# The drive of three of twelve scan units as a product of turned dt*u and diagonal B matrices

## The chip, the cores and the metric

The kernel runs on one core of one Trainium2 chip. The metric is the device time of one execution in microseconds (us), the median over runs. The core has five engines that run side by side, each through its own list of instructions in order: TensorE (PE in the profile, PEld for its weight loads), VectorE (DVE), ScalarE (ACT), GpSimd (POOL), and SyncE (SP), which here only issues DMAs. They meet through semaphores.

## The reference

Eight images of 64 x 64 pixels with 96 channels go through two residual blocks. The time lies in the first one, a selective scan in four directions (K), over L = 4096 positions, for 192 channels d and 16 states n:

```python
def step(h, inp):
    ul, dl, Bl, Cl = inp
    dA = jnp.exp(dl[..., None] * A)
    h = dA * h + (dl * ul)[..., None] * Bl[:, :, None, :]
    y = jnp.einsum('bkdn,bkn->bkd', h, Cl)
    return (h, y)
_, ys = lax.scan(step, h0, (u_t, d_t, B_t, C_t))
```

Here `dl` is a softplus of a projection of the input (dt), `ul` the input u, and B and C are projections too. I call exp(dl*A) the **decay** and (dl*u)*B the **drive**. A normalisation, a convolution and a projection stand ahead of it; behind it come a layer norm, a gate, a projection, and the second block (resampling and a two-layer network with a quadratic).

## The kernel before

Three phases follow one another: `pre_phase` (to about 0.6 ms), `scan_phase` (to about 10.6 ms) and `post_phase`. The change is in `scan_phase` (L309) and in constants that it reads.

**Steps and units.** A step is (image, direction, chunk of TC = 1024 positions, half of the channels): 8 x 4 x 4 x 2 = 256 steps. An even step n and the odd step n+1 are the two halves of one chunk c. A step has 12 units. A unit is 1024 positions for 128 pairs (32 channels, 4 states): channel block j = 0..2, state group g = 0..3. I write x for the unit's place in its step, 0 to 11. Before, g = x // 3 and j = x % 3.

**What one unit takes.**
- the decay, on ScalarE (`exp`, L734): exp of `dlr` (dt, broadcast over states by DMA), scaled by A. It goes to one of 3 buffers `E`.
- the drive. For g = 0..2 (9 of 12 units, x = 0..8) TensorE spreads the group's B over 128 partitions into the PSUM buffer `P[un % 2]` with two matmuls (`fill`, L588 and `spread`, L573), and VectorE multiplies it there by `dur` (dt*u, broadcast by DMA; `multiply`, L651). For g = 3 (x = 9..11, "pooled") GpSimd multiplies `dur` by a copy of B in SBUF (`brep`) into `dbu` (L796), and the decay goes to `P[un % 2]` instead.
- the scan itself, on VectorE: `H = decay*H + drive` along the 1024 positions (`scan`, L671); the last element is carried to the next chunk by ScalarE (`carry`, L740).
- the weighting with C, on GpSimd: `HC = H * crep` (`weigh`, L804), and the sum over states on TensorE (`sum_y`, L609): for each three units and each half of the positions three matmuls with 32 output partitions each, into `yps`.

**What else a step takes.** TensorE projects the chunk (`project`, L557, in even steps) and makes dt (`delta`, L567); ScalarE copies the first (L695, L696) and applies softplus to the second (L705, with a table load on either side); VectorE subtracts once a chunk (`split`, L645); GpSimd makes `dlu` = dt*u (L789); five replicas a chunk (four of C into `crep`, one of B into `brep`) are spread by TensorE (`rep`) into the PSUM area `stage` and copied by ScalarE (L714, L718). `stage` has one job at a time: the table `held` gives for each job the semaphore of the copy that freed it.

**What sets the order.** Each engine has a hand-written loop over un with the jobs placed by x. TensorE issues `fill(un + 1)` first in round un, after `scan_done` says that scan un-1 is done, since that frees `P[(un + 1) % 2]`; then `sum_y` (in two of three rounds) and the job of that x. A block of code that waits holds all behind it on its engine. `H` has 4 buffers, `HC` 7.

## Time and profile before

| | |
|---|---|
| median of 3 runs | 12532.51 us (12529.21 to 12533.41) |
| the profiled execution | 12534.78 us, its span 12533.0 us |
| VectorE busy | 11316.5 us, 90% of the span |
| GpSimd busy | 10322.3 us, 82% |
| TensorE busy | 9868.2 us, 79% |
| ScalarE busy | 6751.2 us, 54% |
| mean granted TensorE clock | 0.759 |

The span is the time from the first to the last instruction; the 1.8 us to the execution's time lie around it. A line of the profile names an engine, a line of the kernel, what it writes and reads, how often, its busy time, the mean of one in ns, and the idle time ahead of it with what ended most of that. The stretch from 2000 to 4000 us, used below, lies wholly in the scan.

### The profile page before, as it was taken

Reading aid. Unit: us, or ns where it says so; the run is one execution under the profiler, and the core shown is the slowest. Engines: PE = TensorE matmul, PEld = TensorE weight load, DVE = VectorE, ACT = ScalarE, POOL = GpSimd, SP = SyncE. Lnnn points to the kernel's source line nnn. Section 1 sums busy time; section 2 is a strip of 40 time slices with the busy share of each in tenths; the row PEclk is TensorE's granted clock in tenths of the full one; section 3 lists DMA queues with packets and bytes.
Section 4 is the critical chain, followed back from the end, with each engine's and each line's share of the span. In section 5 each row is a group of like instructions: output and inputs, shape, how many; then the busy total and the mean of one; then the engine's idle time right before and its main releaser. Section 6 shows DMA issues by size and latency. Waiting matters only on the chain. (4 is left out here: it accounts for less than half of the span.)

```text
span 12533.0 us, 125914 instructions
## 1 busy us (share of the span) xinstructions
PE 9868.2 (79%) x38648; PEld 4005.4 (32%) x38648; DVE 11316.5 (90%) x7318; ACT 6751.2 (54%) x8834; POOL 10322.3 (82%) x4494
## 2 busy tenths in 40 slices
PE   8877777777777777777777777777777776799999
PEld 5622222222222222222222222222222221578878
DVE  7789999999999999999999999999999998555554
ACT  3355555555555555555555555555555554444443
POOL 2189999999999999999999999999999998433330
PEclk9966777677767776777677767776777676799999
DMA  3333343334333333343334333433343333221220
GB/s 106 110 110 112 121 133 112 114 123 133 112 113 120 130 111 114 123 130 112 112 121 130 111 113 121 130 112 116 122 130 111 113 122 105 70 67 48 62 62 11
DMA packets 371523, 1356.57 MB, mean 108 GB/s; under 512 B 47174, under 2 KB 47750, under 8 KB 367532
## 3 DMA queue, kind: packets, MB, share of 16 engines
q1 hardware_dynamic: 370860, 1348.51, 33.5%
q8 instruction: 320, 5.24, 0.2%
q14 instruction: 343, 2.81, 0.1%
HBM read 983.43 MB, written 364.90 MB: 108 GB/s over the span
## 5 line engine op out<-in xcount | busy, mean ns | idle before, releaser
L804 POOL TENSOR_TENSOR HC<-H,crep 128x1024 f32<-128x1024 f32 x3072 | 7196.9, 2361 | 380.1 <-DVE H L671 374.3
L573 PE MATMUL psum<-sx,selb 96*128 96x512 f32 x5888 | 2902.8, 590 | 2096.8 <-DVE H L671 1447.0
L671 DVE TENSOR_TENSOR_SCAN H<-E,car,psum 128x1024 f32<-128x1024 f32 x1728 | 4055.5, 2347 | 61.7
L609 PE MATMUL psum<-HC,sely 128*32 128x512 f32 x12288 | 2957.9, 813 | 9.9 <-POOL HC L804 9.9
L573 PEld LDWEIGHTS psum<-sx,selb 96*128 96x128 f32 x5888 | 1233.2, 256 | 5190.2 <-issue 4295.4
L651 DVE TENSOR_TENSOR psum<-dur,psum 128x1024 f32<-128x1024 f32 x2304 | 2782.0, 1207 | 44.0 <-PE psum L573 43.6
L734 ACT ACTIVATE E<-dlr,am 128x1024 f32<-128x1024 f32 x2304 | 2625.7, 1146 | 322.1 <-DVE H L671 316.6
L796 POOL TENSOR_TENSOR dbu<-dur,brep 128x1024 f32<-128x1024 f32 x768 | 1818.0, 2367 | 0.0
L734 ACT ACTIVATE psum<-dlr,am 128x1024 f32<-128x1024 f32 x768 | 858.7, 1118 | 1653.3 <-DVE H L671 1645.2
L740 ACT COPY car<-H 128x1 f32<-128x1 f32 x2304 | 424.1, 184 | 1891.0 <-DVE H L671 1885.3
L671 DVE TENSOR_TENSOR_SCAN H<-E,psum 128x1024 f32<-128x1024 f32 x576 | 1317.3, 2287 | 21.4 <-ACT E L734 1.5
L671 DVE TENSOR_TENSOR_SCAN H<-psum,car,dbu 128x1024 f32<-128x1024 f32 x576 | 1309.4, 2328 | 3.1
L567 PE MATMUL psum<-dlt,dtw 6*96 6x512 f32 x1024 | 833.5, 957 | 331.2 <-DVE sx L645 330.0
L609 PEld LDWEIGHTS psum<-HC,sely 128*32 128x32 f32 x12288 | 370.6, 125 | 1450.2 <-issue 1304.1
L557 PE MATMUL psum<-u,wx 96*102 96x512 f32 x1024 | 782.9, 900 | 30.1 <-DMA u<-scr_xa 30.1
L789 POOL TENSOR_TENSOR dlu<-dlt,u 96x1024 f32<-96x1024 f32 x256 | 673.1, 2629 | 126.1 <-ACT dlt L705 126.1
L714 ACT COPY crep<-psum 128x1024 f32<-128x1024 f32 x512 | 514.8, 1005 | 164.6 <-PE psum L573 163.7
L1453 POOL TENSOR_TENSOR y<-y,tmp 96x1024 f32<-96x1024 f32 x64 | 194.8, 3089 | 459.2 <-DMA tmp<-scr_yk 459.2
L567 PEld LDWEIGHTS psum<-dlt,dtw 6*96 6x96 f32 x1024 | 210.7, 231 | 787.5 <-DVE sx L645 457.6
L1179 PEld LDWEIGHTS psum<-w2s,hs 128*100 128x100 f32 x4800 | 447.3, 168 | 15.2
L1179 PE MATMUL psum<-w2s,hs 128*100 128x96 f32 x4800 | 447.8, 252 | 0.0
L1464 POOL TENSOR_TENSOR y<-y,szt 96x512 f32<-96x512 f32 x128 | 163.4, 1296 | 323.3 <-ACT y L1342 281.6
(126 smaller groups left out, 9334.5 us busy)
## 6 DMA issues: line engine op xcount, KB each, us to landing
dur<-scr_dlu SPq DMA_DIRECT2D x768, 512.0 KB, 5.3
dlr<-scr_dl SPq DMA_DIRECT2D x768, 512.0 KB, 6.6
scr_dl<-dlt SPq DMA_DIRECT2D x256, 384.0 KB, 3.8
scr_dlu<-dlu SPq DMA_DIRECT2D x256, 384.0 KB, 3.0
scr_yk<-yt SPq DMA_DIRECT2D x256, 384.0 KB, 8.1
yp<-scr_yk SPq DMA_DIRECT2D x128, 384.0 KB, 3.6
scr_xa<-xs SPq DMA_DIRECT2D x64, 384.0 KB, 3.5
scr_sz<-xs SPq DMA_DIRECT2D x64, 384.0 KB, 3.4
```

The lines of the kernel that those rows point to most:

```text
L557: r = e.matmul(stage[0:C + NR, sub * 512:(sub + 1) * 512], wx[:, k, h, :], view(k, h, t0, 512), start=h == 0, stop=h == 1)
L567: r = e.matmul(stage[0:C, sub * 512:(sub + 1) * 512], dtw[C:C + NR, k * ND + half * C:k * ND + (half + 1) * C], dts[:, sub * 512:(sub + 1) ...
L573: r = e.matmul(o[:, sub * 512:(sub + 1) * 512], selb[:, which, :], sx[:, c % 2, sub * 512:(sub + 1) * 512], start=True, stop=True)
L609: r = e.matmul(yps[32 * j:32 * j + 32, cols], sely[:], HC[:, (3 * i + j) % NHC, cols], start=g == 0 and k == 1, stop=g == NG - 1)
L651: e.tensor_tensor(P[un % 2], dur[:, slot(m, j), :], P[un % 2], ALU.mult).then_inc(mul_done)
L671: e.tensor_tensor_scan(H[:, un % NH, ::step], decay[:, ::step], drive[:, ::step], init, ALU.mult, ALU.add).then_inc(scan_done)
L714: e.copy(crep[:, i, :], stage).then_inc(rep_out)
L734: e.activation(o, dlr[:, slot(m, j), :], ACT.Exp, scale=am[:, ae:ae + 1]).then_inc(exp_done)
L789: e.tensor_tensor(shaped(dlu[:], k), shaped(dl, k), view(k, half, t_of(k, ci), TC), ALU.mult).then_inc(dlu_made)
L796: e.tensor_tensor(dbu[:, j, :], dur[:, slot(m, j), :], brep[:], ALU.mult).then_inc(pool_mul_done)
L804: e.tensor_tensor(HC[:, un % NHC, :], H[:, un % NH, :], crep[:, g, :], ALU.mult).then_inc(hc_done)
L1179: r = e.matmul(o[0:NU, i * C:(i + 1) * C], hs[:, q % 2, j, i * NU:(i + 1) * NU], w2s[:, j, :], start=j == 0, stop=j == 2)
```

## The change

Of twelve units of a step, seven now take the drive as before (`DIRECT`), two are `POOLED` (in group g = 1), and three (group g = 3) are `DIAGONAL`: TensorE forms the whole drive. For that
- dt*u of the step (`dlu`, 96 channels x 1024 positions) is turned on TensorE, 128 positions at a time, into `stage` (`turn_dlu`, eight matmuls), and copied by ScalarE into `dluT` (128 x 768);
- the four B rows of group 3 are turned once a chunk (`turn_b`, eight matmuls, a copy of 128 x 32 into `blt`), and ScalarE writes 32 matrices of 128 x 128 a chunk, the identity with its rows scaled by B (`diagonal`);
- `fill` of a diagonal unit is 32 matmuls (8 blocks of 128 positions x 4 states), each with `dluT` (128 x 32) as the weights and a diagonal matrix (128 x 128) as the moving side, writing 32 partitions x 128 of `P`. VectorE's `scan` reads `P` as it is.

To have a state's 32 channels side by side, partitions are now ordered (state, channel) and no longer (channel, state), in the DMAs' broadcast, `selb`, `sely` and `alog`. `ORDER` places the groups so that units without a VectorE multiply alternate with direct ones; of even steps x = 3, 5 are pooled and 7, 9, 11 diagonal, of odd steps 1, 3, 5 are diagonal and 9, 11 pooled. `dbu` has two buffers instead of three. Jobs of `stage` and GpSimd's `delta` have other places, and `dynamic_dma_scratch_size=1024` is given.

```diff
+    NBLK = TC // 128
+    GPOOL, GDIAG = 1, 3
+    DIRECT, POOLED, DIAGONAL = 0, 1, 2
+    ORDER = ((0, 0, 0, 1, 1, 1, 2, 3, 2, 3, 2, 3), (0, 3, 0, 3, 0, 3, 2, 2, 2, 1, 1, 1))
+    KIND = tuple(tuple(DIAGONAL if g == GDIAG else POOLED if g == GPOOL and x in pooled else DIRECT for x, g in enumerate(row))
+                 for row, pooled in zip(ORDER, ((3, 5), (9, 11))))
+    REPS = (0, None, 3, 1, 2)
...
     def tensor(e):
...
+        def turn_b(c):
+            e.wait_ge(*held["bt", c])
+            e.wait_ge(sx_split, c + 1)
+            for k in range(NBLK):
+                r = e.matmul(stage[:, 4 * k:4 * k + 4], sx[:, c % 2, k * 128:(k + 1) * 128], selb[:, 2 * GDIAG, 0:128:32],
+                             start=True, stop=True)
+            r.then_inc(bt_done)
+
+        def turn_dlu(m, sub):
+            if sub == 0:
+                e.wait_ge(*held["lt", m])
+                e.wait_ge(dlu_made, m + 1)
+            for k in range(NBLK // 2):
+                t0 = (sub * (NBLK // 2) + k) * 128
+                r = e.matmul(stage[:, sub * 512 + k * C:sub * 512 + (k + 1) * C], dlu[:, t0:t0 + 128], idn[0:C, 0:C],
+                             start=True, stop=True)
+            if sub:
+                r.then_inc(lt_done)
 
         def fill(un):
-            if un >= NUNIT or on_pool(un):
+            if un >= NUNIT or kind(un) == POOLED:
                 return
-            m, g = un // 12, un % 12 // 3
-            e.wait_ge(sx_split, m // 2 + 1)
+            b, k, ci, half, m, g, j = place(un)
             if un >= 2:
                 e.wait_ge(scan_done, un - 1)
-            spread(P[un % 2], m // 2, 2 * g).then_inc(fill_done)
+            if kind(un) == DIRECT:
+                e.wait_ge(sx_split, m // 2 + 1)
+                spread(P[un % 2], m // 2, 2 * g).then_inc(fill_done)
+            else:
+                e.wait_ge(lt_copied, m + 1)
+                e.wait_ge(diag_made, NBLK * 4 * (m // 2 + 1))
+                for i in range(NBLK):
+                    for q in range(4):
+                        r = e.matmul(P[un % 2][32 * q:32 * q + 32, i * 128:(i + 1) * 128],
+                                     dluT[:, m % 2, i, 32 * j:32 * j + 32], diag[:, i, q, :], start=True, stop=True)
+                r.then_inc(fill_done)
...
             if n % 2 == 0:
-                if x < 3 and n and n < NSTEP:
+                if x < 3 and n:
                     rep(c - 1, x + 2)
-                if x in (4, 7) and c < NCHUNK:
-                    project(c, x // 7)
-                if x == 10 and c < NCHUNK:
+                if x in (3, 4):
+                    turn_dlu(n + 1, x - 3)
+                if x in (5, 7) and c < NCHUNK:
+                    project(c, (x - 5) // 2)
+                if x == 9 and c < NCHUNK:
                     delta(n + 2)
-            else:
-                if x == 4 and c < NCHUNK:
+            elif c < NCHUNK:
+                if x == 1:
+                    turn_b(c)
+                if x == 3:
                     delta(n + 2)
-                if x in (8, 10) and c < NCHUNK:
+                if x in (6, 7):
+                    turn_dlu(n + 1, x - 6)
+                if x in (8, 10):
                     rep(c, (x - 8) // 2)
...
     def scalar(e):
...
+        def diagonal(c, first, n):
+            if first == 0:
+                e.wait_ge(bt_copied, c + 1)
                 if c:
-                    e.wait_ge(pool_mul_done, 3 * 2 * c)
-                e.copy(brep[:], stage).then_inc(rep_out)
+                    e.wait_ge(fill_done, fills(last_of(2 * c - 1, kinds=(DIAGONAL,))) + 1)
+            for i in range(first, first + n):
+                e.mul(diag[:, i // 4, i % 4, :], idn[:], blt[:, i:i + 1]).then_inc(diag_made)
...
-            if x == 1 and 2 <= n + 1 < NSTEP and not ends_image(n + 1):
-                delta(n + 1)
-            if x in (3, 5, 7):
-                multiply(n, (x - 3) // 2)
-            if x == 7 and n + 2 < NSTEP and ends_image(n + 2):
-                delta(n + 2)
+            if n % 2 == 0:
+                if x in (0, 2):
+                    multiply(12 * n + 3 + x)
+            else:
+                if x == 0 and n + 1 < NSTEP:
+                    delta(n + 1)
+                if x in (3, 5):
+                    multiply(12 * n + 6 + x)
+                if x == 8 and n + 2 < NSTEP:
+                    delta(n + 2)
```

TensorE's list at the middle of an even step, before. `psum<-sx,selb` is a spread, `psum<-u,wx` a half of `project`, `psum<-yp,idn` and `psum<-HC,sely` belong to `sum_y`, `psum<-dlt,dtw` is `delta`.

```order
L573 MATMUL psum<-sx,selb 128x512 x2
L557 MATMUL psum<-u,wx 102x512 x2
L573 MATMUL psum<-sx,selb 128x512 x2
L603 MATMUL psum<-yp,idn 96x512
L609 MATMUL psum<-HC,sely 32x512 x3
L573 MATMUL psum<-sx,selb 128x512 x2
L603 MATMUL psum<-yp,idn 96x512
L609 MATMUL psum<-HC,sely 32x512 x3
L573 MATMUL psum<-sx,selb 128x512 x2
L557 MATMUL psum<-u,wx 102x512 x2
L609 MATMUL psum<-HC,sely 32x512 x6
L567 MATMUL psum<-dlt,dtw 96x512 x2
```

The same place after the change, from round x = 3 of an even step on (`psum<-idn,dlu` is `turn_dlu`, `psum<-diag,dluT` the fill of a diagonal unit):

```order
L624 MATMUL psum<-idn,dlu 128x96 x8
L601 MATMUL psum<-sx,selb 128x512 x2
L659 MATMUL psum<-yp,idn 96x512
L665 MATMUL psum<-HC,sely 32x512 x3
L585 MATMUL psum<-u,wx 102x512 x2
L643 MATMUL psum<-diag,dluT 32x128 x32
L659 MATMUL psum<-yp,idn 96x512
L665 MATMUL psum<-HC,sely 32x512 x3
L601 MATMUL psum<-sx,selb 128x512 x2
L585 MATMUL psum<-u,wx 102x512 x2
L643 MATMUL psum<-diag,dluT 32x128 x32
```

The first half of `project` now stands behind the spread and the first `sum_y` of the step and directly ahead of a diagonal fill; so does the second half.

ScalarE's list in the first half of an even step, before (`E<-dlr,am` is `exp`, `car<-H` a carry, `yt<-psum` the copy of y):

```order
L718 COPY brep<-psum 128x1024
L734 ACTIVATE E<-dlr,am 128x1024
L740 COPY car<-H 128x1
L746 COPY yt<-psum 96x1024
L734 ACTIVATE E<-dlr,am 128x1024
L740 COPY car<-H 128x1
L734 ACTIVATE E<-dlr,am 128x1024
L740 COPY car<-H 128x1
```

After:

```order
L824 ACTIVATE psum<-dlr,am 128x1024
L830 COPY car<-H 128x1
L836 COPY yt<-psum 96x1024
L808 ACTIVATE diag<-idn,blt 128x128 x2
L824 ACTIVATE E<-dlr,am 128x1024
L830 COPY car<-H 128x1
L808 ACTIVATE diag<-idn,blt 128x128 x2
L799 COPY dluT<-psum 128x768
L824 ACTIVATE E<-dlr,am 128x1024
L830 COPY car<-H 128x1
L808 ACTIVATE diag<-idn,blt 128x128 x2
```

Diagonal matrices stand in each round here, and the copy of `dluT` behind them in round x = 5; the last two matrices of the chunk are in round x = 6.

## Rows read from the trace of the kernel before

**Rows 1.** The page: span, and busy time of each engine.

```profile
span 12533.0 us, 125914 instructions
PE 9868.2 (79%) x38648; PEld 4005.4 (32%) x38648; DVE 11316.5 (90%) x7318; ACT 6751.2 (54%) x8834; POOL 10322.3 (82%) x4494
```

**Rows 2.** The page: TensorE's granted clock in 40 slices of the span.

```profile
PEclk9966777677767776777677767776777676799999
```

**Rows 3.** Windows of the scan: length, busy PE PEld DVE ACT POOL, clock, DMA, GB/s.

```profile
2000.00:4000.00 2000.00, 1503.85 (x4204) 438.96 (x4202) 1977.25 (x1105) 1143.86 (x1472) 1926.28 (x823) 0.71 0.35 117
5031.50:5038.00 6.50, 6.24 (x10) 2.90 (x10) 6.43 (x5) 3.39 (x5) 6.50 (x4) 0.50 0.80 257
5038.50:5045.00 6.50, 6.41 (x28) 2.07 (x31) 6.43 (x4) 1.43 (x3) 6.50 (x4) 1.00 0.20 61
```

**Rows 4.** The page: the multiply on VectorE, over the whole span.

```profile
L651 DVE TENSOR_TENSOR psum<-dur,psum 128x1024 f32<-128x1024 f32 x2304 | 2782.0, 1207 | 44.0 <-PE psum L573 43.6
```

**Rows 5.** Groups of instructions from 2000 to 4000 us.

```profile
L804 POOL TENSOR_TENSOR HC<-H,crep 128x1024 f32<-128x1024 f32 x617 | 1445.8, 2361 | 73.7 <-DVE H L671 72.5
...
L651 DVE TENSOR_TENSOR psum<-dur,psum 128x1024 f32<-128x1024 f32 x462 | 557.8, 1207 | 3.8 <-PE psum L573 3.7
L734 ACT ACTIVATE E<-dlr,am 128x1024 f32<-128x1024 f32 x460 | 524.3, 1146 | 60.4 <-DVE H L671 59.2 <-issue 0.2
L796 POOL TENSOR_TENSOR dbu<-dur,brep 128x1024 f32<-128x1024 f32 x155 | 367.1, 2368 | 0.0
...
L789 POOL TENSOR_TENSOR dlu<-dlt,u 96x1024 f32<-96x1024 f32 x51 | 133.4, 2616 | 0.0
L714 ACT COPY crep<-psum 128x1024 f32<-128x1024 f32 x101 | 101.6, 1006 | 30.7 <-PE psum L573 30.6
L740 ACT COPY car<-H 128x1 f32<-128x1 f32 x472 | 86.9, 184 | 387.9 <-DVE H L671 386.7
```

**Rows 6.** VectorE in order of time: start, us, line, what, count.

```profile
5021.19 1.21 DVE L651 TENSOR_TENSOR psum<-dur,psum 128x1024 f32<-128x1024 f32 x1
5022.43 2.29 DVE L671 TENSOR_TENSOR_SCAN H<-E,psum 128x1024 f32<-128x1024 f32 x1
5024.64 1.21 DVE L651 TENSOR_TENSOR psum<-dur,psum 128x1024 f32<-128x1024 f32 x1
```

**Rows 7.** TensorE in order of time; in brackets the idle time ahead.

```profile
4999.65 1.93 PE L609 MATMUL psum<-HC,sely 128*32 128x512 f32 x6
...
5028.94 1.06 PE L609 MATMUL psum<-HC,sely 128*32 128x512 f32 x6
5031.76 1.19 PE L573 MATMUL psum<-sx,selb 96*128 96x512 f32 x2 [1.75 <-DVE H L671]
...
5039.42 0.74 PE L573 MATMUL psum<-sx,selb 96*128 96x512 f32 x2
5040.00 1.02 PE L603 MATMUL psum<-yp,idn 96*96 96x512 f32 x2
5040.95 1.06 PE L609 MATMUL psum<-HC,sely 128*32 128x512 f32 x6
...
5042.63 1.88 PE L557 MATMUL psum<-u,wx 96*102 96x512 f32 x4
```

**Rows 8.** Short matmuls on TensorE in the last phase, in order of time.

```profile
10978.39 0.90 PE L1137 MATMUL psum<-ut,x 64*64 64x100 f32 x16
...
11317.56 1.46 PE L1161 MATMUL psum<-ut,t 64*64 64x100 f32 x20
...
11321.09 2.81 PE L1179 MATMUL psum<-w2s,hs 128*100 128x96 f32 x30
```

**Rows 9.** Groups on ScalarE from 10800 us on, with small operands.

```profile
L1393 ACT COPY t<-psum 128x400 f32<-128x400 f32 x42 | 20.7, 492 | 72.2 <-PE psum L1137 72.2
...
L1384 ACT ACTIVATE b1a<-b1p,co 128x1 f32<-128x1 f32 x21 | 6.6, 378 | 28.1 <-DVE b1p L1275 28.1
```

**Rows 10.** Waits from 2000 to 4000 us: total us, times, longest.

```profile
DVE psum L651 <- PE psum L573: 3.7, 10, 0.6
...
DVE sx L645 <- ACT sx L696: 0.9, 2, 0.5
```

More of the change, by code:

```diff
@@ L336, in scan_phase @@
     dlu = T("dlu", [C, TC])
+    blt = T("blt", [128, NBLK * 4])
+    diag = T("diag", [128, NBLK, 4, 128])
+    dluT = T("dluT", [128, 2, NBLK, C])
     sx = T("sx", [C, 2, TC], F32R)
@@ L393, in shaped, with kind, tally, fills @@
         return ap if k % 2 == 0 else ap.rearrange("p (w h) -> p w h", h=HW)
-    def unit_of(m, g, j):
-        return 12 * m + 3 * g + j
     def place(un):
         m, x = divmod(un, 12)
-        return steps[m] + (m, x // NJ, x % NJ)
-    def on_pool(un):
-        return un % 12 >= 3 * GB
-    def a_index(un):
-        return 9 * (un // 12) + un % 12
-    def a_unit(a):
-        return 12 * (a // 9) + a % 9
+        return steps[m] + (m, ORDER[m % 2][x], x % NJ)
+    def kind(un):
+        return KIND[un // 12 % 2][un % 12]
+    def tally(un, *kinds):
+        c, r = divmod(un, 24)
+        return c * sum(KIND[p][x] in kinds for p in range(2) for x in range(12)) + sum(kind(i) in kinds for i in range(r))
+    def fills(un):
+        return tally(un, DIRECT, DIAGONAL)
+    def muls(un):
+        return tally(un, DIRECT)
+    def pooled(un):
+        return tally(un, POOLED)
+    def last_of(m, **want):
+        return max(un for un in range(12 * m, 12 * m + 12)
+                   if want.get("g", place(un)[5]) == place(un)[5] and want.get("j", un % 3) == un % 3
+                   and kind(un) in want.get("kinds", (DIRECT, POOLED, DIAGONAL)))
+    filled = [un for un in range(NUNIT) if kind(un) != POOLED]
+    pooled_units = [un for un in range(NUNIT) if kind(un) == POOLED]
     def slot(m, j):
@@ L602, in sum_y @@
                 e.wait_ge(yp_in, 16 * (seconds(m) + 1))
-                r = e.matmul(yps[0:C, cols], idn[:], yp[:, cols], start=True, stop=False)
+                r = e.matmul(yps[0:C, cols], idn[0:C, 0:C], yp[:, cols], start=True, stop=False)
                 if sub:
@@ L618, in tensor @@
         delta(0)
+        turn_b(0)
+        turn_dlu(0, 0)
+        turn_dlu(0, 1)
         delta(1)
@@ L683, in vector @@
             c = n // 2 + 1
-            if not on_pool(un):
+            if kind(un) == DIRECT:
                 multiply(un)
@@ L755, in scalar @@
         delta(0)
+        turn_b(0)
+        turn_dlu(0)
         delta(1)
@@ L760, in scalar @@
         exp(0)
+        diagonal(0, 0, 18)
         for un in range(NUNIT + 12):
@@ L766, in scalar @@
                 carry(un - 1)
+            if x == 4 and n:
+                copy_y(n - 1)
+            if n == NSTEP:
+                continue
             if n % 2 == 0:
-                if 1 <= x <= 3 and n and n < NSTEP:
+                if 1 <= x <= 3 and n:
                     rep(c - 1, x + 1)
+                if x < 7:
+                    diagonal(c - 1, 18 + 2 * x, 2)
+                if x == 5:
+                    turn_dlu(n + 1)
                 if x == 8 and c < NCHUNK:
                     project(c)
-                if x == 11 and c < NCHUNK:
+                if x == 10 and c < NCHUNK:
                     delta(n + 2)
-            else:
-                if x == 5 and c < NCHUNK:
+            elif c < NCHUNK:
+                if x == 2:
+                    turn_b(c)
+                if x == 5:
                     delta(n + 2)
-                if x in (9, 11) and c < NCHUNK:
+                if x == 7:
+                    turn_dlu(n + 1)
+                if x in (9, 11):
                     rep(c, (x - 9) // 2)
-            if x == 4 and n:
-                copy_y(n - 1)
+                if x >= 6:
+                    diagonal(c, 3 * (x - 6), 3)
     def pool(e):
```

113 lines of the change are left out of this document (70 added, 43 removed).

## The prediction, made before the changed kernel ran

> **What bounds the kernel now.** I read the page's totals first, then the windows of the scan, then the groups, then the order of time. VectorE is the busiest engine over the span [rows 1], but that is a mean over phases; from 2000 to 4000 us it is busy 1977.25 of 2000 us, GpSimd 1926.28, TensorE 1503.85, ScalarE 1143.86 [rows 3]. VectorE waits there for TensorE's fill only 3.7 us in ten places [rows 10]. So the scan phase is VectorE's own work end to end. The multiplies count the steps: 462 in 2000 us, nine a step, give 51.3 steps of 38.97 us, of which VectorE idles 0.44 us. 256 steps are 9976 us.
>
> GpSimd is close behind: twelve weightings of 2.361, three multiplies of 2.368 and one dlu of 2.616 [rows 5] are 38.1 us a step by durations. The change must take from both, and it does.
>
> TensorE is the engine to watch. Its clock stands at 0.71 in the scan [rows 3] and near 1.0 in the first and last phase [rows 2], so it runs part of the scan at 1.2 GHz and part at 2.4 (at 0.5 and 1.0, a mean of 0.71 is 58% of the time at the lower). One sum of three matmuls takes 1.93 us at the one and 1.06 at the other [rows 7].
>
> **What is taken away.** VectorE loses two of nine multiplies a step: 512 in all, by 1.207 us [rows 4], is 618 us. (By starts the multiply costs 1.24, 5021.19 to 5022.43 [rows 6]; I keep the duration.) The scans stay, and a diagonal unit reads its drive from PSUM as a direct one does. GpSimd loses one of three multiplies: 12 x 2.361 + 2 x 2.368 + 2.616 = 35.7 us a step. VectorE's new step is 38.97 - 2.41 = 36.56 us, so GpSimd stays below. Its places matter too: an odd step now has two dlu (38.3 us of work), an even one none (33.1). Followed unit by unit with starts at each scan's end, GpSimd is some 6 us behind at the end of the odd step and catches up in the even one. `H` lets it be about three units (9 us) behind, and `sum_y` two to three; I cost this at nothing, covered by the even step's slack of 3.5 us.
>
> **The diagonal fill.** 32 matmuls, fp32, so 64 instructions by the trace's habit of two records each. The nearest row is `sum_y`: six instructions of 512 columns on three sets of 32 output partitions take 1.06 us [rows 7], where four of 512 columns on one set take 1.88, or 0.43 each: the three sets work side by side, in two turns of 0.43 plus 0.2 for the way out. With four sets and 128 columns, the fill is 16 turns of 0.107 plus 0.2: 1.9 us at 2.4 GHz; at 1.2 GHz 16 x 0.213 + 0.2 = 3.6. A short-matmul row supports it: sixteen of 100 columns, two sets, 0.90 us [rows 8], (0.90 - 0.2)/8 = 0.09 a turn. I take 2.1 with its issue. The bounds: 1.8 below, and above, if the four sets go one after another, 64 x 0.107 = 6.8, near the 0.09 of L1179's instructions on one set (thirty in 2.81 [rows 8]).
>
> May it be late? The fill may start when scan un-2 ends; ahead of the scan that needs it VectorE has the direct neighbour's multiply and scan, 3.45 us by starts [rows 6]. That is what alternating the kinds does. At 2.4 GHz 2.1 fits, with 1.3 us left for whatever TensorE still has; at 1.2 GHz 3.6 does not quite.
>
> **TensorE's sum** for a step at 2.4 GHz, by spacing of starts: seven spreads of 0.6 are 4.2; three diagonal fills 6.3; eight sums of 0.95 (5040.00 to 5040.95 and the like) 7.6; skip or earlier y, two of 0.95 in three of four steps, 1.4; half a project and a delta, four instructions of 0.43 each, 3.4; two and a half replicas 1.5; `turn_dlu`, 16 instructions of 0.094, 1.5; `turn_b` 0.4. Together 26.3 of 36.6 us. At 1.2 GHz it would be about 52: more than a step. So TensorE cannot stay at the low clock; its clock in the scan must rise, to some 0.85 or 0.9 by my estimate, since the full rows after 5038.5 [rows 3] follow a dense stretch at half clock and the change makes stretches dense.
>
> **Where VectorE will wait.** Set t = 0 at the end of scan 4 in an even step. Scan 7 is due at 2.27 + 3.45 = 5.7. TensorE meets: the spread 0.65, earlier y 0.95, the sum 0.95, half of project 1.7 (it also waits for the copy of `dluT`: on ScalarE a carry 0.2, two diagonals 0.6, the copy 0.8, so 1.6 to 2.1, earlier than TensorE gets there); the diagonal fill starts at 4.3 and ends at 6.4. Wait 0.7. The next one (x = 9) has sum, spread and the other half of project ahead, 0.3 to 0.5 late; `split` 0.1; the third, behind `delta`, is saved by the split's 1.2. In the odd step each diagonal has 0.3 to 1 us to spare. That is 1.2 us for two steps at the full clock.
>
> But between rounds 3 and 5 TensorE idles about 2.6 us. After an idle time of 1.75 us the rows from 5031.76 on run at 0.50, for 6.5 us of steady work [rows 3, 7]. If that happens here, 6.5 us yield 3.3 and the fill ends at 9.6: a wait of 3.9 instead of 0.7, 4.4 in all. I take 2.3 for two steps, between these ends, because the clock was low only 58% of the time with the old density, and the denser lists should hold it up more often. 128 x 2.3 = 294 us, bounds 154 and 563.
>
> **ScalarE.** 16 diagonals a step. A copy of one column is 0.184 and of 1024 1.006 [rows 5]; a one-column ACTIVATE with operands read from a tile 0.378, a copy of 400 columns 0.492 [rows 9]. I take 0.39, about 0.3 by spacing (bounds 0.2 and 0.5): 4.8 a step, plus 0.8 for the copy of `dluT` and little else. It was 1143.86 / 51.3 = 22.3, and becomes 28 of 37 us. Hidden, as long as no copy that TensorE waits for comes late; the last two matrices are written 0.2 + 0.6 us after scan 5, before TensorE reaches fill 7. If the diagonals cost 0.5, 3 us more a step still fit. The DMAs move the same bytes with another order of rows; none is waited for by VectorE: nothing. Eighteen diagonals ahead of the first unit cost 5 us, once.
>
> **Sum.** 12534.8 - 618 + 294 + 5 = 12216 by the profiled execution; it lies 2.3 over the median, so 12214. I say 12210.
>
> **Rivals.**
> (1) The low clock at each first diagonal fill, 4.4 to 5 us for two steps: 12534 - 618 + 563 to 640, 12480 to 12556. For it: the idle 2.6 us ahead, longer than the 1.75 of the row. Against: density. It is centred on no change.
> (2) Slower: the diagonal fill is bound by its number of instructions. Twenty short ones of L1161 take 1.46 us, 0.063 each without the 0.2 [rows 8], though two sets were at work. At that pace 64 take 4.0 + 0.1. Against the window of 3.45 each fill is 0.65 late by itself; with what stands ahead of them, x = 7 is 2.7 late, x = 9 2.5, x = 11 0.5, and the odd step's 0.65, 0.65 and, behind `delta`, 2.0: 9 us for two steps, 1152 in all: 13070. It turns to slower once a fill takes about 3.1 us at the full clock. For it: no row has 64 such instructions in a run. Against: L1137's sixteen go at 0.044. Sets that don't overlap (6.8) would give 26.3 + 14.1 = 40.4 us a step on TensorE, at least 12534 + 256 x 1.4 = 12900, and belong here.
> The Trainium skill ("TensorE: Matmul & The Clock Gate", "Wait — 56ns, not 53.3ns?") has a rule for this: with hardware decoding off, the sequencer takes about 62 ns a matmul, and that binds when the array's work is shorter. By it the fill would be 64 x 62 ns = 4.0 us, an estimate, and the time this rival's. L1137's row is faster than that, but sixteen may have been decoded beforehand, so the trace doesn't settle it.
> (3) ScalarE works in order; table loads, diagonals and copies pile up, and its exp or copy is late by 1 to 2 us a step: 12214 + 256 or 512, 12470 to 12730. For it: 28 us in pieces that wait for others. Against: it has 9 us a step to spare.
> (4) All at the full clock and all hidden: 12534 - 618 + 0 to 154, 11916 to 12070.
>
> **How the numbers follow.** Forecast 0.50 (12100 to 12330), rival 4 0.10, rival 1 0.15 (a third each way), rival 3 0.09, rival 2 0.16. Faster by over 0.2% (25 us, about what a measurement can tell): 0.50 + 0.10 + 0.06 + 0.05 = 0.71; same 0.06; slower 0.23. The range holds the forecast, most of rival 4, rival 1 and more than half of 3: 11960 to 12680.
>
> **What would show it.** In the profile after: 1792 multiplies on VectorE instead of 2304, at 1.207; the diagonal's fill near 2 us from its first to its last start at clock 1.00; waits of VectorE's scan for the diagonal fill, near 0.7 us or more, once in two steps at x = 7; the clock of the scan at 0.85 or more; ScalarE near 28 us a step. The prediction is wrong if a diagonal fill takes over 3 us at the full clock, if VectorE waits at all six diagonal units of two steps, if ScalarE or GpSimd ends its waits, or if the clock stays near 0.7.

## The result, and the profile after

| | before | after |
|---|---|---|
| time, median (us) | 12,533.0 | 13,066.3 |
| lowest to highest | 12,529.2 to 12,536.1 | 13,056.9 to 13,069.2 |
| span of the profiled execution | 12,533.0 | 13,055.0 |
| granted clock from 2000 to 4000 us | 0.71 | 0.83 |

The change makes the kernel slower: the ratio is 1.0424, 95% interval 1.0406 to 1.0442, or 533 us. The prediction was 12,210 in a range of 11,960 to 12,680; both its sign and its range were wrong. The number of its slower rival, 13,070, is close to the result, but it is not that rival's mechanism: at the full clock the fills are as short as forecast.

The page of the kernel after: span, busy time, and the groups that the prediction speaks of (columns as in [rows 1, 4, 5]).

```profile
span 13055.0 us, 236757 instructions
PE 10838.8 (83%) x91896; PEld 5733.0 (44%) x91896; DVE 10740.7 (82%) x6806; ACT 8110.9 (62%) x13314; POOL 9754.9 (75%) x4238
...
L718 DVE TENSOR_TENSOR psum<-dur,psum 128x1024 f32<-128x1024 f32 x1792 | 2169.4, 1211 | 308.6 <-DMA dur<-scr_dlu 158.0
...
L808 ACT ACTIVATE diag<-idn,blt 128x128 f32<-128x128 f32 x4096 | 1375.5, 393 | 1.5 <-issue 0.8
```

VectorE does 1792 multiplies instead of 2304, as intended, and is busy 576 us less than in [rows 1]. Its idle time grew by more. L718 is the multiply (L651 before), L740 the scan (L671 before), L601 the spread, L712 the split, L643 the fill from diagonals, L808 the writing of one diagonal on ScalarE.

Waits of the kernel after from 2000 to 4000 us, all engines (total us, times, longest). In [rows 10] VectorE's whole list for the same stretch is 4.6 us.

```profile
DVE H L740 <- PE psum L643: 95.1, 40, 5.4
DVE psum L718 <- DMA dur<-scr_dlu: 33.8, 15, 4.6
DVE psum L718 <- PE psum L601: 21.8, 33, 1.2
DVE sx L712 <- ACT sx L765: 20.3, 23, 1.9
...
ACT E L824 <- DMA dlr<-scr_dl: 140.6, 59, 6.9
...
SPq L514 <- DMA scr_dlu<-dlu: 507.3, 50, 17.6
```

Two things are new. One was foreseen, with its place: the scan waits for a fill from diagonals (95.1 us, 40 times, up to 5.4). The other was not: VectorE and ScalarE wait for the broadcasts `dur` and `dlr`, and the queue that issues them waits up to 17.6 us for a write to the scratch in DRAM. The page's DMA issues (KB each, median us from issue to landing) show how long such a write takes now:

```profile
scr_dl<-dlt SPq DMA_DIRECT2D x256, 384.0 KB, 15.2
scr_dlu<-dlu SPq DMA_DIRECT2D x256, 384.0 KB, 13.1
```

The same two writes took 3.8 and 3.0 us in the kernel before. Nothing about them was changed; what was changed is what stands around them in the queues, the broadcasts. A window of 10 us of before, then one of after (columns as in [rows 3], the DMA share is the last but one):

```profile
5070.00:5080.00 10.00, 9.61 (x19) 2.70 (x16) 9.89 (x7) 8.01 (x10) 10.00 (x5) 0.50 0.95 346
```

```profile
5050.00:5060.00 10.00, 8.84 (x153) 6.51 (x150) 9.75 (x6) 4.84 (x10) 10.00 (x5) 0.83 0.24 82
```

Before, the broadcasts came in bursts on nearly all 16 DMA engines (share 0.95, 346 GB/s). In the window of after the share is a quarter, and the rate 82 GB/s. The bytes moved over the whole execution are the same.

**The fill from diagonals** itself, in TensorE's order of time in the kernel after: the first ran with the clock changing in it (granted clock 0.61 over its row), the second at 1.00, the third mostly at 0.50 (0.53).

```profile
5031.16 3.09 PE L643 MATMUL psum<-diag,dluT 128*32 128x128 f32 x64
...
5039.12 1.96 PE L643 MATMUL psum<-diag,dluT 128*32 128x128 f32 x64
...
5050.69 3.55 PE L643 MATMUL psum<-diag,dluT 128*32 128x128 f32 x64 [0.52 <-DVE H L740]
```

### The profile page after: what moved, and what is told of

Read it like the earlier page. It is cut to its first block and busy times, and to the rows that moved or that the text cites. A ratio compares the mean times of both kernels' runs of the same rounds, so it can differ in the third digit from the quotient of the medians.

```text
span 13055.0 us, 236757 instructions
## 1 busy us (share of the span) xinstructions
PE 10838.8 (83%) x91896; PEld 5733.0 (44%) x91896; DVE 10740.7 (82%) x6806; ACT 8110.9 (62%) x13314; POOL 9754.9 (75%) x4238
## 3 DMA queue, kind: packets, MB, share of 16 engines
q14 instruction: 373, 3.05, 0.1%
## 5 line engine op out<-in xcount | busy, mean ns | idle before, releaser
L740 DVE TENSOR_TENSOR_SCAN H<-E,car,psum 128x1024 f32<-128x1024 f32 x1920 | 4473.4, 2343 | 597.1 <-PE psum L643 374.8
L601 PE MATMUL psum<-sx,selb 96*128 96x512 f32 x4864 | 2161.8, 541 | 1709.9 <-DVE H L740 1114.6
L824 ACT ACTIVATE E<-dlr,am 128x1024 f32<-128x1024 f32 x2560 | 2922.2, 1146 | 1026.2 <-DMA dlr<-scr_dl 784.2
L601 PEld LDWEIGHTS psum<-sx,selb 96*128 96x128 f32 x4864 | 940.7, 237 | 3538.7 <-DVE H L740 1961.3
L718 DVE TENSOR_TENSOR psum<-dur,psum 128x1024 f32<-128x1024 f32 x1792 | 2169.4, 1211 | 308.6 <-DMA dur<-scr_dlu 158.0
L643 PE MATMUL psum<-diag,dluT 128*32 128x128 f32 x49152 | 1724.9, 300 | 166.4 <-DVE H L740 165.6
L643 PEld LDWEIGHTS psum<-diag,dluT 128*32 128x32 f32 x49152 | 1477.4, 121 | 865.5 <-DVE H L740 529.2
L740 DVE TENSOR_TENSOR_SCAN H<-E,psum 128x1024 f32<-128x1024 f32 x640 | 1453.6, 2283 | 205.4 <-PE psum L643 151.5
L808 ACT ACTIVATE diag<-idn,blt 128x128 f32<-128x128 f32 x4096 | 1375.5, 393 | 1.5 <-issue 0.8
L904 POOL TENSOR_TENSOR dbu<-dur,brep 128x1024 f32<-128x1024 f32 x512 | 1213.6, 2370 | 2.4 <-ACT brep L781 2.4
L740 DVE TENSOR_TENSOR_SCAN H<-psum,car,dbu 128x1024 f32<-128x1024 f32 x384 | 894.2, 2329 | 10.7 <-ACT psum L824 9.5
L624 PEld LDWEIGHTS psum<-idn,dlu 96*128 96x128 f32 x4096 | 558.4, 212 | 275.8 <-issue 212.4
L624 PE MATMUL psum<-idn,dlu 96*128 96x96 f32 x4096 | 600.3, 301 | 0.6 <-POOL dlu L895 0.6
## 6 DMA issues: line engine op xcount, KB each, us to landing
scr_dl<-dlt SPq DMA_DIRECT2D x256, 384.0 KB, 15.2
```

What stands on the lines that cost most here:

```text
L601: r = e.matmul(o[:, sub * 512:(sub + 1) * 512], selb[:, which, :], sx[:, c % 2, sub * 512:(sub + 1) * 512], start=True, stop=True)
L624: r = e.matmul(stage[:, sub * 512 + k * C:sub * 512 + (k + 1) * C], dlu[:, t0:t0 + 128], idn[0:C, 0:C], start=True, stop=True)
L643: r = e.matmul(P[un % 2][32 * q:32 * q + 32, i * 128:(i + 1) * 128], dluT[:, m % 2, i, 32 * j:32 * j + 32], diag[:, i, q, :], start=True, ...
L718: e.tensor_tensor(P[un % 2], dur[:, slot(m, j), :], P[un % 2], ALU.mult).then_inc(mul_done)
L740: e.tensor_tensor_scan(H[:, un % NH, ::step], decay[:, ::step], drive[:, ::step], init, ALU.mult, ALU.add).then_inc(scan_done)
L808: e.mul(diag[:, i // 4, i % 4, :], idn[:], blt[:, i:i + 1]).then_inc(diag_made)
```

## The experiments

Two causes stood open after this profile. **D**: the new order of the replicated rows. The broadcast's destination was 32 groups of 4 partitions, and is now 4 groups of 32; by this theory a transfer whose outer dimension is 4 runs on 4 of the 16 DMA engines, where 32 runs on all. **C**: the wait for TensorE at x = 7 of the even step, made large by the low clock. Against D stood a smaller scratch area for the DMA descriptors, which the change also brings (theory S in the expectations). Theory T of the expectations is C in its first wording. Two rivals of C come with e5: theory L, that it is the amount of work ahead of the fill at whatever clock, and theory A, that ScalarE's diagonals and copies are late. All ratios are to the kernel before, measured on the same chip, with a 95% interval.

### e1: the change with the old form of the broadcast

```
-  .unsqueeze(0).to_broadcast([4, 32, TC])     (in_dur and in_dlr)
+  .unsqueeze(1).to_broadcast([32, 4, TC])
```

> The changed kernel with one thing undone: the DMAs that broadcast dl and dlu into dlr and dur read 32 rows four times each, as before ([32, 4, 1024]), and no longer 4 x 32 rows. The rows land in other partitions than the rest expects, so the output is not the reference's; bytes, instructions and waits are the same. Theory D (the broadcast with 4 as its outer dimension runs on a quarter of the 16 DMA engines, and its lateness is passed on through ScalarE to TensorE): landing of scr_dl back from 15.2 us to about 4, no wait of ScalarE's exp for dlr, time 12150 to 12400. Theory S (the small scratch for DMA descriptors slows all DMAs): the stores keep 13 to 20 us to landing, time stays near 13066. Theory T (TensorE at half clock ahead of the first diagonal fill is the cause, the DMAs are a bystander): landings recover but the time stays above 12850, with waits of about 5 us before the scan at x = 7.

The rows now land in partitions that the matrices and the decay don't expect, so this kernel computes something else with the same amount of work. Measured: 12,653.3 us, ratio 1.0096 (1.0081 to 1.0111). 413 us come back. `scr_dl` lands in 3.9 us again, `scr_dlu` in 3.2, `dur` in 5.4. The time lies between the two that D alone (up to 12,400) and T alone (over 12,850) were to give: VectorE still waits 113.2 us in 2000 for the diagonal fills, up to 6.5 at a time. Both causes are at work.

### e2: the change with four plain DMAs of 32 rows for each broadcast

The counts that are waited for go with it, 64 for each broadcast instead of 16.

```
-  e.dma_start(dur[:, slot(m, j), :], S["dlu"][m % 2, 32*j:32*j+32, :].unsqueeze(0).to_broadcast([4, 32, TC]))
+  for q in range(4):
+      e.dma_start(dur[32*q:32*q+32, slot(m, j), :], S["dlu"][m % 2, 32*j:32*j+32, :])
```

> The changed kernel with each broadcast issued as four plain DMAs of 32 rows x 4 KB (24 a step instead of 6), output as the reference. Theory D: each DMA has 32 rows as its outer dimension and uses the DMA engines as before, so the time is near that of the old broadcast, 12150 to 12450; the issue takes SyncE 24 x 0.6 = 14 us of 37 a step, which could cost some of it. Theory S and theory T: near 13066.

Measured: 12,649.9 us, ratio 1.0090 (1.0075 to 1.0105), again above the 12,450 expected at most. The same bytes go to the same partitions as in the changed kernel, and the kernel is 416 us shorter. The transfers land in 3.2 and 3.6 us; no wait for a DMA is left among VectorE's in this stretch, and what is left is the other cause:

```profile
2000.00:4000.00 2000.00, 1704.87 (x14830) 791.95 (x14831) 1838.85 (x993) 1406.97 (x2348) 1791.90 (x764) 0.83 0.45 116
```

```profile
DVE H L740 <- PE psum L643: 114.8, 46, 5.4
...
DVE sx L712 <- ACT sx L765: 20.4, 24, 1.9
...
DVE psum L718 <- PE psum L601: 5.7, 18, 0.4
```

I keep e2's form in e5 to e7 and e9 to e12: it is free of cause D.

### e3: the kernel before with the smaller scratch area for descriptors

```
-  nc = _bacc.Bacc("TRN2", target_bir_lowering=False, num_devices=1)
+  nc = _bacc.Bacc("TRN2", target_bir_lowering=False, num_devices=1, dynamic_dma_scratch_size=1024)
```

> The kernel before with only dynamic_dma_scratch_size=1024 added. Theory D and theory T: 12533, within 0.2%, landings as before (3 to 8 us). Theory S: landings of 13 to 20 us and over 12700.

Measured: 12,535.1 us, ratio 1.0002 (0.9992 to 1.0011). It costs nothing.

### e4: the kernel before with only the new order of rows

```
-  .unsqueeze(1).to_broadcast([32, 4, TC])     (in_dur and in_dlr)
+  .unsqueeze(0).to_broadcast([4, 32, TC])
-  p = (d * 4 + ni).ravel()                    (the matrices that spread and sum)
+  p = (ni * 32 + d).ravel()
-  A_logs ... .transpose(3, 5, 0, 1, 2, 4)
+  A_logs ... .transpose(5, 3, 0, 1, 2, 4)
```

> The kernel before with only the new order of partitions (DMA broadcast [4, 32, 1024], selb, sely and alog to match), output as the reference. Theory D: landings of scr_dl and scr_dlu rise to 10 us and more, DMA share about 0.25 whenever a broadcast runs; a step moves 6 x 512 KB at about 100 GB/s = 31 us of 39 in one queue, so it is slower than 12533, by my estimate 12650 to 13100. Theory S: 12533. Theory T: 12533 within 0.5%, since TensorE has slack here.

Measured: 13,100.5 us, ratio 1.0455 (1.0440 to 1.0471), at the upper end of what was expected. Without one diagonal, the order of the rows alone costs the old kernel 568 us. The old kernel's TensorE has no new work here, so D stands by itself; that it is the transfers, and not the new order in the matrices, e2 shows, which keeps that order. A window from inside a broadcast of e4, and its waits in the stretch from 2000 us on:

```profile
5005.00:5010.00 5.00, 5.00 (x11) 1.20 (x10) 4.93 (x4) 4.87 (x5) 5.00 (x4) 0.50 0.25 99
```

```profile
ACT E L734 <- DMA dlr<-scr_dl: 185.2, 61, 8.7
...
DVE psum L651 <- DMA dur<-scr_dlu: 43.0, 35, 2.1
```

A share of 0.25 of 16 engines is four engines, at 99 GB/s together, some 25 each.

### e8: the change with two broadcasts of two groups

```
+  for q in range(2):
+      e.dma_start(dur[64*q:64*q+64, ...], S["dlu"][...].unsqueeze(0).to_broadcast([2, 32, TC]))
```

> The changed kernel with each broadcast as two DMAs whose outer dimension is 2 ([2, 32, 1024]) where it has one of 4. Theory D in its strict form (the number of DMA engines that work on a transfer is its outer dimension, and the transfers of the queue follow one another): a DMA share near 2/16 = 0.13 while a broadcast runs and some 60 GB/s, so a step's 3 MB take over 50 us: 15000 us or more. If two such transfers run side by side: a share of 0.25 and about 13066. If the outer dimension has nothing to do with it: 12650.

Measured in a single execution: 20,648.7 us, span 20,646.9. It moves the same bytes as e2 and puts them in the same partitions. The windows:

```profile
5020.00:5030.00 10.00, 9.68 (x62) 4.48 (x54) 9.41 (x6) 5.24 (x13) 6.87 (x4) 1.00 0.13 52
5040.00:5050.00 10.00, 4.27 (x14) 0.70 (x8) 2.49 (x2) 0.00 (x0) 4.41 (x2) 0.52 0.13 52
```

0.13 of 16 is two engines, at 52 GB/s. The number of engines follows the outer dimension: 2 gives two, 4 gives four. The two DMAs of a broadcast don't share out over other engines either, or the share would be 0.25: SyncE issues the six for `dur` in 15.50 us and waits for nothing between them, while 1.57 MB at 52 GB/s take 30, so several are under way together. In e2 each piece has 32 rows as its outer dimension and lands fast. The Trainium skill states this rule ("DMA: Bandwidth & Descriptors", "Why a DMA increments its semaphore by 16 and not by 1"): the number of engines is the largest one up to 16 that divides the slowest dimension, other than 1, of both sides, and on a hardware queue, as SyncE's is here, they are the lowest-numbered ones. The shares of e4 and e8 agree with the first half; that e8's DMAs stay on the same two engines agrees with the second, though no view here shows which two they are.

### e5: TensorE given more to do

Replicas spread three times, and the direct fills from x = 7 of an odd step to x = 5 of an even one twice. Only work is added to e2; the last spread writes what the first did.

```
-  for sub in range(2):
+  for sub in [0, 1] * times:                   # times = 3 for replicas
...
-  spread(P[un % 2], m // 2, 2 * g).then_inc(fill_done)
+  spread(P[un % 2], m // 2, 2 * g, 2 if (un % 24) >= 19 or (un % 24) < 6 else 1).then_inc(fill_done)
```

> e2 (the changed kernel with four plain DMAs for each broadcast) with TensorE given more to do where it idles: each replica is spread three times over into the same place, and the direct fills of rounds x = 7 on of odd steps and up to x = 5 of even steps twice; same output. Theory C (VectorE waits at x = 7 because TensorE comes there at 1.2 GHz after thin rounds): the granted clock in the scan rises from 0.83 to over 0.9, waits of VectorE's scan for the diagonal fill fall from 114.8 us in 2000 to under 60, time from 12650 to 12300 to 12480, though there is more work. Theory L (it is the amount of work queued ahead of that fill, at whatever clock): no gain, 12650 to 12800. Theory A (ScalarE's diagonals and copies come late): no change, within 30 us of 12650.

Measured: 12,513.2 us, ratio 0.9982 (0.9973 to 0.9992); 137 us less than e2 by work that is only added. The granted clock of the scan rose from 0.83 to 0.92, and VectorE's wait for the diagonals fell from 114.8 to 77.7 us in 2000. The direction is C's and neither L's nor A's, but the gain is smaller than C was to give (12,480 at most, a wait under 60):

```profile
2000.00:4000.00 2000.00, 1779.31 (x15911) 921.32 (x15906) 1870.53 (x1010) 1425.46 (x2387) 1826.54 (x777) 0.92 0.46 119
```

### e6 and e7: the projection moved away from the stall

e6 takes e2 and brings the halves of `project` from x = 5 and 7 to x = 3 and 4, `turn_dlu` from 3 and 4 to 9 and 10, `delta` from 9 to 7 and the split from behind scan 8 to behind scan 5, with ScalarE's copies to match. e7 adds e5's extra work to it.

```
-  if x in (3, 4): turn_dlu(n + 1, x - 3)
-  if x in (5, 7) and c < NCHUNK: project(c, (x - 5) // 2)
-  if x == 9 and c < NCHUNK: delta(n + 2)
+  if x in (3, 4) and c < NCHUNK: project(c, x - 3)
+  if x == 7 and c < NCHUNK: delta(n + 2)
+  if x in (9, 10): turn_dlu(n + 1, x - 9)
```

> e2 with the jobs of the staging area in another order in even steps: both halves of project in rounds 3 and 4, its copies and VectorE's split at x = 5, delta in round 7 (softplus at 8), the turns of dlu in rounds 9 and 10 (copy at 11), the last diagonals by x = 4; same work, same output. Theory L: nothing stands between the first sum of the step and the fill of x = 7, none between x = 7 and 9 but delta, so VectorE's waits fall by more than half: 12300 to 12450. Theory C: the work before the fill is the same in sum and still runs at the low clock, so the wait at x = 7 stays; the 0.8 us of split's wait and x = 9's go: 12480 to 12580. Theory A: depends on when ScalarE's last diagonal is written; earlier by two rounds here, so 12450 or less with ScalarE no longer late.

> e5 and e6 together. If theories C and L each hold a part, the gains add: 12100 to 12350, below both kernels. If only C holds, as e5; if only L, as e6 or slower.

Measured: e6 12,483.8 us, ratio 0.9955 (0.9940 to 0.9970), above L's 12,450 and just inside C's 12,480 to 12,580; e7 12,504.9, ratio 0.9970 (0.9960 to 0.9980), so the gains do not add. The wait for the diagonals is nearly gone in e6, and another has come: VectorE's split waits for ScalarE's copy of the projection, which TensorE gives late, at the low clock by my reading (e12 tests it). VectorE's waits in e6, then in e7:

```profile
DVE sx L713 <- ACT sx L766: 82.2, 26, 4.5
DVE H L741 <- PE psum L644: 21.1, 35, 1.6
```

```profile
DVE sx L713 <- ACT sx L766: 71.4, 26, 5.2
DVE H L741 <- PE psum L644: 32.8, 50, 2.5
```

The extra work of e5 added in e7 raised the clock of the whole execution from 0.84 to 0.91 and gained nothing: what it took from the one wait it gave to the other. I read this as work beyond what the thin places need getting in the way itself; e12 adds less and gains, but no run shows which of e7's additions is too much.

### e9: the split moved back by two units

```
-  if x == 7 and c < NCHUNK: delta(n + 2)             (e6)
+  if x == 8 and c < NCHUNK: delta(n + 2)
-  if c < NCHUNK and n % 2 == 0 and x == 5: split(c)
+  if c < NCHUNK and n % 2 == 0 and x == 7: split(c)
```

ScalarE's copies of the projection and its softplus come one unit later as well, at x = 6 and 9.

> e6 with the copies of project on ScalarE at x = 6 (was 5), VectorE's split behind scan 7 (was 5), delta in round 8 and softplus at 9 (was 7 and 8); same work and output. In e6 the waits at x = 7 went and 3.5 us a chunk appeared at the split instead. If that was only the split's place in VectorE's list, ahead of what it needs, it goes and nothing takes its place: 12483 - 128 x 3.0 = 12100, within 12060 to 12250. If TensorE's work ahead of fill 7 at the low clock is what counts wherever the split stands, the wait is back at x = 7 to 9 and the time stays at 12400 to 12500.

Measured: 12,627.9 us, ratio 1.0072 (1.0055 to 1.0089). This missed both ranges that were expected: the split's wait is gone, but 144 us are lost against e6. TensorE now stands in the way of the fills again:

```profile
DVE H L741 <- PE psum L644: 79.3, 40, 2.7
DVE psum L719 <- PE psum L602: 58.3, 23, 3.3
```

and both halves of the projection, in one row of TensorE's order of time, take 7.12 us at the low clock (3.68 in e10's row):

```profile
5072.34 7.12 PE L586 MATMUL psum<-u,wx 96*102 96x512 f32 x8
```

### e10: e9 with each replica spread twice

```
-  spread(stage, c, 2 * GPOOL if REPS[i] is None else 2 * REPS[i] + 1).then_inc(rep_done)
+  spread(stage, c, 2 * GPOOL if REPS[i] is None else 2 * REPS[i] + 1, 2).then_inc(rep_done)
```

> e9 with each replica spread twice over (five times two more matmuls a chunk), nothing else. If the low clock still costs something in e9, the clock rises from about 0.83 towards 0.87 and the time falls by 10 to 60 us; if TensorE has slack enough in e9, it is the same as e9 within 0.2%.

Measured: 12,468.5 us, ratio 0.9950 (0.9933 to 0.9967): 159 us less than e9, where 10 to 60 were expected, with nothing changed but five instructions more a step, whose result is what stood there already (1246 of L602 in 2000 us instead of 970). The granted clock in the stretch went from 0.80 to 0.87, VectorE's wait for the diagonals from 79.3 to 72.2 us and that for the spreads from 58.3 to 36.2, and the projection's row to half:

```profile
5074.90 3.68 PE L586 MATMUL psum<-u,wx 96*102 96x512 f32 x8
```

### e11 and e12: the same addition in the order of the change, and with the projection early

The edit of e10, in e2 and in e6.

> The change with its four plain DMAs of 32 rows (12,650 us) and one thing more: each replica of a C row is spread twice by TensorE, so only work is added, about 2 x 0.48 us of it per replica and 10 replicas in two steps, in the thin rounds. Theory C (what the wait at x = 7 costs is the low clock that TensorE has when it comes to the blocks of the diagonals, and more work ahead of it keeps the clock up): the granted clock of the scan rises from 0.83 to about 0.87, and the time falls by 100 to 160 us, to 12,490 to 12,550, as between the two kernels with the later split (-160) and as when the direct fills were spread twice too (-137). Rival: the work there is what is late, whatever the clock; then the added 5 us in two steps make the wait longer, and the time rises to 12,700 to 12,900. Range 12,490 to 12,620.

> The kernel with the projection early (12,484 us, where VectorE waits 4.5 us in 26 of 50 steps for ScalarE's copy of the projection, which TensorE gives late at the low clock, and little for the diagonals), with each replica spread twice and nothing else changed. Theory C: with the clock held up ahead of the projection, that copy comes 1.5 to 2 us sooner; 128 x 1.5 to 2 us is 190 to 250 us, so 12,240 to 12,300. Rival: the clock there does not follow the replicas, or the copy is late by ScalarE's own queue; then 12,450 to 12,510, as when the direct fills were spread twice too (12,505). Range 12,240 to 12,500.

Measured: e11 12,442.3 us, ratio 0.9928 (0.9913 to 0.9942), 208 us less than e2 and below the 12,490 that I expected at best. e12 12,363.5 us, ratio 0.9864 (0.9847 to 0.9880), 120 us less than e6, where 190 to 250 were expected; the split's wait fell from 82.2 to 58.3 us and did not go. e11, then e12, from 2000 to 4000 us:

```profile
2000.00:4000.00 2000.00, 1680.07 (x15362) 800.00 (x15366) 1885.43 (x1018) 1441.63 (x2410) 1843.26 (x785) 0.90 0.46 120
```

```profile
DVE H L740 <- PE psum L643: 69.1, 36, 5.6
DVE sx L712 <- ACT sx L765: 20.4, 24, 1.9
```

```profile
2000.00:4000.00 2000.00, 1734.47 (x15357) 846.38 (x15360) 1879.51 (x1016) 1437.82 (x2396) 1834.43 (x781) 0.86 0.46 120
```

```profile
DVE sx L713 <- ACT sx L766: 58.3, 23, 4.8
DVE H L741 <- PE psum L644: 34.2, 34, 2.5
```

(In e12, as in e6, e7, e9 and e10, the same lines are numbered one higher.) In e11 TensorE is busy 1680.07 us of the stretch, in e2 1704.87, though it has more to do: the added work is paid by the clock. Both kernels are faster than before and after; e12 is the best of this study.

## Why the prediction was wrong

**The sum, with what was measured in its place.** The rows of VectorE's multiplies, scans and splits over the whole span, added up in each kernel (busy, and idle just ahead of them):

| kernel | busy | idle | span less both |
|---|---|---|---|
| before | 10,045.5 | 161.2 | 2,326 |
| after | 9,437.4 | 1,262.1 | 2,356 |
| e2 | 9,432.0 | 853.5 | 2,333 |
| e11 | 9,429.2 | 677.0 | 2,337 |
| e12 | 9,422.8 | 604.9 | 2,337 |

The last column hardly moves, so two terms tell the time. The saving is 608 us busy (forecast 618, right). The idle time grew by 1101, where I had 294. Of that 409 is D (after less e2; by the times 416), and 692 is the rest, e2 less before. In e2 the page puts 416.8 + 149.0 = 566 us of idle time to the diagonal fills, 134 to the split (30.0 in before), 59 to the spreads (44 in before). So: 12,533 - 608 + 692 + 409 + 30 = 13,056, the span. The last term is the table's last column; it has no cause that I have found. Without D the time would have been e2's 12,650, inside the range near its upper end, but still slower than the kernel before and not faster.

**The step that failed first** is "The DMAs move the same bytes with another order of rows; none is waited for by VectorE: nothing". It priced an edit by its bytes and not by its shape. Neither a landing time nor the share of the DMA engines enters it, and no rival held it. It cost 409 us of 12,533 in the changed kernel (e1 and e2 give 413 and 416 back) and 568 in the old one (e4). Nor is "none is waited for by VectorE" so: over the span of after its multiply waits 158.0 us for `dur`, 74 times (250.0 us, 204 times, in e4). ScalarE waits longer, 784.2 us for `dlr`, and only part of that reaches VectorE. Of the 409 us, after less e2, VectorE's list names 158 for `dur`, 87 more for the spreads and 53 more for the exp; 133 stand ahead of scans with no releaser named, and the wait for the diagonals is 40 less. The place to look was the window at 0.95 above: a burst that uses nearly all engines has something to lose by its shape.

**The step that was mis-sized** is "I take 2.3 for two steps, between these ends". Over e2's 128 pairs of steps, the idle time that was added is 692 / 128 = 5.4 us a pair. The upper bound, 4.4, was too low as well; with 5.4 in place of 2.3 and no D the sum would have been 12,613, against 12,621 of e2's profiled execution, the shortest of its four (median 12,650). Rival 1, "the low clock at each first diagonal fill", is what happened in e2, and was underpriced. Its mechanism can be followed in e2 in TensorE's order of time:

```profile
5064.73 0.84 PE L601 MATMUL psum<-sx,selb 96*128 96x512 f32 x2 [2.26 <-ACT crep L787]
...
5067.10 1.93 PE L665 MATMUL psum<-HC,sely 128*32 128x512 f32 x6
5068.95 3.73 PE L624 MATMUL psum<-idn,dlu 96*128 96x96 f32 x16
5072.39 1.20 PE L601 MATMUL psum<-sx,selb 96*128 96x512 f32 x2
5073.39 1.91 PE L659 MATMUL psum<-yp,idn 96*96 96x512 f32 x2
5075.23 1.93 PE L665 MATMUL psum<-HC,sely 128*32 128x512 f32 x6
5077.09 2.82 PE L585 MATMUL psum<-u,wx 96*102 96x512 f32 x4
5079.84 1.96 PE L643 MATMUL psum<-diag,dluT 128*32 128x128 f32 x64
```

and in VectorE's:

```profile
5074.89 2.29 DVE L740 TENSOR_TENSOR_SCAN H<-E,psum 128x1024 f32<-128x1024 f32 x1
5081.86 2.29 DVE L740 TENSOR_TENSOR_SCAN H<-E,psum 128x1024 f32<-128x1024 f32 x1 [4.68 <-PE psum L643]
```

The list is the one forecast: spread, earlier y, sum, half of the projection, fill. At the full clock it is 0.6 + 0.95 + 0.95 + 1.9 + 1.95 = 6.35 from the end of scan 4, where 5.75 are there: 0.6, about the forecast's 0.7. But it starts 0.96 late (5072.39, where VectorE's scan 5 starts at 5071.43, right behind scan 4), because the turns of `dlu` ahead of it took 3.73 us instead of the 2.02 of e11's row; I had counted `turn_dlu` in the sum for the step and not in this chain. The spread, y, sum and projection then take 7.45 where 4.4 would do at the full clock, 3.05 more. 0.6 + 0.96 + 3.05 = 4.6, against the wait of 4.68.

The low stretch was longer than I had allowed. I took the 6.5 us of [rows 3] for its length. For that place of the kernel before this is nearly right: finer windows have the clock full up to 5031.0 and again from 5038.0. It is not the length at this place of e2, where the clock falls at about 5065.2 and is full again at 5078.8, 13.6 us:

```profile
5067.00:5078.50 11.50, 11.50 (x35) 5.57 (x35) 10.11 (x6) 10.14 (x20) 11.50 (x6) 0.50 0.12 36
5078.50:5082.00 3.50, 3.50 (x68) 2.10 (x67) 0.14 (x1) 0.00 (x0) 1.88 (x1) 0.95 0.00 0
```

TensorE was busy 11.50 of 11.50 us at 0.50. The idle time is not where the forecast had it either, 2.6 us between rounds 3 and 5: it is 2.26 us at 5064.73, ahead of a replica, and 0.38 behind that, and from 5067.10 on there is none. "The denser lists should hold it up more often" held for the mean, which rose from 0.71 to 0.83 (0.85 or more was forecast), and failed at this fill: the denser lists are those of the units with diagonals, and they stand behind the thin rounds, not in them.

**That the clock is the price** e10, e11 and e12 show: two matmuls added to each replica, where TensorE had idled, take 120 to 208 us off the whole, in three orders of the work. e11 in the same place, with a short low stretch (granted clock 0.63 from 5069.50 to 5073.50, 0.97 from there to 5082.00) instead of a long one at 0.50, in TensorE's order of time; its wait there is 2.32:

```profile
5069.74 0.73 PE L601 MATMUL psum<-sx,selb 96*128 96x512 f32 x2 [2.07 <-DVE H L740]
5070.31 1.66 PE L659 MATMUL psum<-yp,idn 96*96 96x512 f32 x2
5071.90 1.93 PE L665 MATMUL psum<-HC,sely 128*32 128x512 f32 x6
5073.76 2.04 PE L585 MATMUL psum<-u,wx 96*102 96x512 f32 x4
5075.74 1.95 PE L643 MATMUL psum<-diag,dluT 128*32 128x128 f32 x64
```

Here 1.66 and 1.93 are the low clock's, 1.6 us too much together, and 2.32 less 1.6 is again the forecast's 0.7. The addition saves 208 us of e2's 692; the clock still falls in some places. How much of the rest is the clock's is open (the split's 104 us more than before are not, as said below): no kernel here ran the whole scan at the full clock.

**The split** waits 134 us over the span (forecast 0.1 for two steps, 13 in all; before 30). It stands behind ScalarE's copies of the projection, which wait for the second half. This is not the clock's: the wait is 134.3 us in e2, 133.4 in e5 and 133.9 in e11, whose clocks differ, and at this place of e2 (5081.00 to 5088.00) the granted clock is 1.00. There the half of the projection starts at 5084.31, behind the fill, the earlier y, the sum and the spread, and takes 1.88; ScalarE's two copies take 1.01 each behind it; VectorE, done with scan 8, waits 0.22. So the chain ends behind scan 8 at the full clock too; on average over e2 the wait is 1.05 us (134.3 / 128), where the forecast had 0.1.

**What was right.**
- The fill's length: forecast 1.9 to 2.1 at the full clock and 3.6 at half; measured 1.95 to 1.96, and 3.55 in the row mostly at half clock. The four sets work side by side.
- Rival 2, a fill bound by the number of its instructions, is refuted: 64 in 1.95 us are 0.030 each. The Trainium skill's figure for a sequencer without hardware decoding ("TensorE: Matmul & The Clock Gate", "Wait — 56ns, not 53.3ns?"), 62 ns a matmul, does not bind these 64; by it the fill would be 4.0, an estimate. (Counted on the program's 32 matmuls it would be 2.0, an estimate too, and that the rows don't tell from the 1.95.) That the result came to within 4 us of this rival's number is chance: D, which it had not, makes up the difference.
- Rival 3: ScalarE's diagonal is 0.393 (forecast 0.39), and L808's idle time over the span of after is 1.5 us. From 2000 to 4000 us of e2 it is busy 1406.97 us in 50.7 steps (355 multiplies, seven each), 27.8 a step, where 28 was forecast. No diagonal was late by ScalarE's doing: in after and in e2 all of L643's named waits are for VectorE's scan. ScalarE ends 4.7 us of the waits of VectorE's scan in e2. The late copies of e6 and e7 I put down to TensorE, since an addition to TensorE's work alone shortens the wait for them in e12.
- GpSimd costs next to nothing: in after it waits 265.7 us in 2000 for VectorE's scan, and in e2 VectorE waits for it six times over the span, 21.0 us.
- The place: one large wait in two steps, x = 7 of the even one. Averaged over e2, VectorE idles 4.1 us there, 0.9 at x = 9 with the split, and 0.4 or less at any other unit.

## What to carry to other kernels

When a change touches the shape of a transfer, price it by the number of DMA engines that its outer dimension reaches, read as the DMA share in a window of a few us, and not by its bytes. When a change gives work to an engine whose clock varies, cost the chain ahead of its first consumer at the low level from the first instruction behind the last idle place on, and look whether work ahead of it, even work that is thrown away, would close that place. A wait that is moved by another order goes to the next consumer of the same late chain: e6 and e9 took the stall from the fill to the split and back, while e10 to e12 shortened it.
